# Low parts of the weights of layers 1 and 2: subtracted by GpSimd instead of DVE

## What is computed

```python
for i in range(n_layers):                       # 3 layers of 200 outputs
    z = jnp.einsum('bmd,bnd->bmnd', x, hidden).reshape(B, -1, D)
    cur = jnp.einsum('bcd,co->bod', z, Ws[i]) + bs[i][None, :, None]
    cur = jax.nn.relu(cur)
    if SPLIT_HALF and i != n_layers - 1:        # half goes on, half goes out
        hidden, direct = (cur[:, :half, :], cur[:, half:, :])
    else:
        direct = cur
        hidden = cur
    finals.append(direct)
return jnp.sum(jnp.concatenate(finals, axis=1), axis=-1)
```

## Time and profile before

| | |
|---|---|
| median of 3 runs | 2704.21 us (2703.4 to 2704.91) |
| the profiled execution | 2704.38 us |
| its span, first to last instruction | 2702.6 us |
| mean granted TensorE clock | 0.996 of full speed |
| TensorE busy | 2671.3 us, 99% |
| DVE busy | 2641.8 us, 98% |
| ScalarE busy | 1677.6 us, 62% |
| GpSimd busy | 3.3 us |

### The profile page before, as it was taken

How to read it: one execution, slowest core, us unless ns; L and a number is a source line. 1 busy time by engine, 2 the same in 40 slices (tenths; PEclk the granted TensorE clock), 3 DMA queues, 4 the chain that set the end, 5 groups by cost and what they waited for, 6 DMA issues and landing times.

```text
span 2702.6 us, 52144 instructions
## 1 busy us (share of the span) xinstructions
PE 2671.3 (99%) x17992; PEld 2658.1 (98%) x17992; DVE 2641.8 (98%) x2731; ACT 1677.6 (62%) x2853; POOL 3.3 (0%) x9
## 2 busy tenths in 40 slices
PE   6999999999999999999999999999999999999999
PEld 4999999999999999999999999999999999999999
DVE  6999999999999999999999999999999999999998
ACT  5666666666666666666666666666666666666664
POOL 0000000000000000000000000000000000000000
PEclk8999999999999999999999999999999999999999
DMA  8554444444554454444455444444444454445442
GB/s 196 131 145 129 110 115 131 121 110 123 135 139 112 127 131 110 114 130 123 112 134 142 121 110 125 130 113 113 129 127 114 119 133 118 110 125 130 112 110 63
DMA packets 230130, 332.65 MB, mean 123 GB/s; under 512 B 27976, under 2 KB 165172, under 8 KB 229940
## 3 DMA queue, kind: packets, MB, share of 16 engines
q1 hardware_dynamic: 230038, 331.46, 47.0%
HBM read 326.67 MB, written 6.60 MB: 123 GB/s over the span
## 4 chain that ended last, share of the span: by engine, by line
PE 97%; issue 1%; DVE 0%; DMA 0%; ACT 0%; SPq 0%; POOLq 0%; POOL 0%; ACTq 0%; DVEq 0%
PE acc L850 61%; PE acc L851 28%; PE acc L843 6%; PE turned L863 1%; PE x_turned L885 1%; PE x_turned L872 0%; DMA xb<-x_by_unit 0%; DVE z_low L483 0%; DVE w_split L434 0%; DMA mixed<-in_r_x_dram 0%; SPq L255 0%; ACT w_split L715 0%; DVE z L478 0%; ACT mixed L711 0%; POOLq L109 0%
## 5 line engine op out<-in xcount | busy, mean ns | idle before, releaser
L850 PE MATMUL acc<-w_split,z_high 128*128 128x400 f32 (+1 forms) x8320 | 2490.9, 367 | 19.4 <-DVE z_low L483 16.0
L851 PE MATMUL acc<-w_split,z_low 128*128 128x200 f32 (+1 forms) x8320 | 2119.4, 255 | 0.0
L851 PEld LDWEIGHTS acc<-w_split,z_low 128*128 128x128 f32 (+1 forms) x8320 | 1591.6, 191 | 0.0
L850 PEld LDWEIGHTS acc<-w_split,z_high 128*128 128x128 f32 (+1 forms) x8320 | 1564.0, 188 | 21.9 <-issue 16.4
L680 ACT ACTIVATE z_high<-z 128x1024 fp32r<-128x1024 f32 (+3 forms) x1152 | 1113.3, 976 | 693.2 <-DVE z L478 583.8
L483 DVE TENSOR_TENSOR z_low<-z,z_high 128x1024 fp32r<-128x1024 f32 (+3 forms) x1152 | 1284.7, 1115 | 26.5 <-PE acc L851 24.1
L478 DVE TENSOR_TENSOR z<-mixed,xb 128x1024 f32<-128x1024 f32 (+2 forms) x1024 | 1211.6, 1183 | 0.0
L705 ACT ACTIVATE mixed<-turned 32x128 f32<-32x128 f32 x768 | 205.5, 268 | 8.8
L843 PE MATMUL acc<-w_whole,z 128*128 128x200 f32 x1024 | 196.7, 335 | 0.8 <-DVE s L497 0.8
L843 PEld LDWEIGHTS acc<-w_whole,z 128*128 128x128 f32 x1024 | 168.1, 190 | 1.1 <-DVE s L497 1.1
L702 ACT ACTIVATE mixed<-turned 96x512 f32<-96x512 f32 x256 | 151.2, 590 | 6.9 <-PE turned L863 2.0
(11 more groups left out here) (27 smaller groups left out, 76.3 us busy)
## 6 DMA issues: line engine op xcount, KB each, us to landing
xb<-x_by_unit SPq DMA_DIRECT2D x378, 384.0 KB, 4.2
x_right<-x_by_unit SPq DMA_DIRECT2D x384, 136.5 KB
xb<-x_by_unit SPq DMA_DIRECT2D x384, 128.0 KB, 4.9
xb<-x_by_unit SPq DMA_DIRECT2D x126, 336.0 KB
xb<-x_by_unit SPq DMA_DIRECT2D x128, 84.0 KB
x_left<-x_by_unit SPq DMA_DIRECT2D x384, 19.5 KB
mixed<-in_L_rec_W_dram SPq DMA_DIRECT2D x5, 600.0 KB, 5.7
x_by_unit<-mixed SPq DMA_DIRECT2D x16, 160.0 KB, 2.9
```

Source lines behind the costliest of these rows:

```text
L850: nc.tensor.matmul(a[:, 0:2 * O], z_high[slot % HIGH_RING][0:rows, tok], w, start=(c == 0), stop=False, skip_group_check=True)
L851: last = nc.tensor.matmul(a[:, 0:O], z_low[slot % RING][0:rows, tok], w[:, 0:O], start=False, stop=(c == chunks - 1), skip_group_check=True)
```

## The change

The eight low parts of the weights of layers 1 and 2 are taken out of DVE's written order and put on GpSimd, between and around the two memsets of the staging buffer. The subtraction is the same, on the same tiles. DVE keeps the low part of the weights of layer 0. The orders of TensorE, ScalarE and SP are as before, and the counts keep their meaning.

```diff
--- before.py
+++ after.py
@@ -420,11 +420,24 @@
             pool.wait_ge(consts_step, 1)
             nc.gpsimd.affine_select(out=ident, in_=ident, compare_op=ALU.not_equal, fill=1.0,
                                     base=0, pattern=[[-1, P]], channel_multiplier=1).then_inc(consts, 1)
+            def low_piece(i, l, g):
+
+                pool.wait_ge(w_high_done, i + 1)
+                pool.wait_ge(w_low_done, i)
+                w = piece(l, g)
+                nc.gpsimd.tensor_tensor(w[:, :, O:2 * O], stage(l, g), w[:, :, 0:O].bitcast(F32), ALU.subtract).then_inc(w_low_done, 1)
+
+            pool.wait_ge(w_low_done, 1)
             for l in range(1, 3):
-
-                pool.wait_ge(w_low_done, 4 * l - 1)
+                at = GROUPS * (l - 1) + 1
+                low_piece(at, l, 0)
+                low_piece(at + 1, l, 1)
+
+                pool.wait_ge(w_low_done, at + 2)
                 nc.gpsimd.memset(stage(l, GROUPS - 1)[MAIN:P, :, :], 0.0).then_inc(stage_ready, 1)
-
+                pool.wait_ge(stage_ready, l)
+                low_piece(at + 2, l, 2)
+                low_piece(at + 3, l, 3)
 
         @block.vector
         def _(dve):
@@ -432,9 +445,6 @@
 
                 dve.wait_ge(w_high_done, i + 1)
                 nc.vector.tensor_tensor(w[:, :, O:2 * O], st, w[:, :, 0:O].bitcast(F32), ALU.subtract).then_inc(w_low_done, 1)
-
-            def low_piece(i, l, g):
-                low_w(i, piece(l, g), stage(l, g))
 
             def ones(i):
                 nc.vector.memset(xb[i][MAIN:P, TAIL_AT:CHUNKS, :], 1.0).then_inc(ones_set, 1)
@@ -548,11 +558,9 @@
             dve.wait_ge(w_low_done, 1)
             product0(0, 0, 0)
             lows(0, 0, L0_ROWS, L0_CHUNKS)
-            low_piece(1, 1, 0)
             sums(0, 1, 1, None)
             dve.wait_ge(s_in, 1)
             fresh(0, 1).then_inc(direct_in, 1)
-            low_piece(2, 1, 1)
 
 
             at = first(0)
@@ -565,21 +573,18 @@
             lows(at + 1, at + 1, P, group_chunks(1))
             sums(0, 1, 2, 1)
             product12(1, 0, 0, 3, at + 3, at + 3)
-            low_piece(3, 1, 2)
             product0(2, at + GROUPS, at + GROUPS)
             dve.wait_ge(s_in, 2)
             dve.wait_ge(direct_in, 1)
             add(0, 1).then_inc(direct_in, 1)
             lows(at + 2, at + 2, P, group_chunks(2))
             lows(at + 3, at + 3, P, group_chunks(3))
-            low_piece(4, 1, 3)
             lows(at + GROUPS, at + GROUPS, L0_ROWS, L0_CHUNKS)
 
 
             at = first(1)
             product12(1, 1, 1, 0, at, at)
             product12(1, 1, 1, 1, at + 1, at + 1)
-            low_piece(5, 2, 0)
             product12(1, 1, 1, 2, at + 2, at + 2)
             lows(at, at, P, group_chunks(0))
             sums(0, 2, ended(0), 2)
@@ -587,8 +592,6 @@
             product12(1, 1, 1, 3, at + 3, at + 3)
             lows(at + 2, at + 2, P, group_chunks(2))
             product0(3, at + 4, at + 4)
-            low_piece(6, 2, 1)
-            low_piece(7, 2, 2)
             lows(at + 3, at + 3, P, group_chunks(3))
             lows(at + 4, at + 4, L0_ROWS, L0_CHUNKS)
             product12(2, 0, 0, 0, at + 5, at + 5)
@@ -600,7 +603,6 @@
             product12(2, 0, 0, 3, at + 8, at + 8)
             sums(0, 2, ended(1), 3)
             lows(at + 7, at + 7, P, group_chunks(2))
-            low_piece(8, 2, 3)
 
             def period(r, d, n, base, sl):
```

## The result

The changed kernel takes 2719.82 us, median of 6 runs (2712.28 to 2720.53), against 2703.95 for the kernel before on the same chip: ratio 1.0052, 95% interval 1.0042 to 1.0062. It is 15.9 us slower. The six runs lie at two levels: 2712.28 and 2713.12, and four from 2719.75 to 2720.53. The forecast of 2712 was the lower level; most runs are on the upper one, outside the range. The profiled execution (2719.75 us, span 2717.9) is of the upper level.

What follows compares the result with a forecast made beforehand. TensorE runs without a break after a prologue up to 85.79 us, so only that start's shift counts. GpSimd and DVE shutting each other out move it by 8 us: 2704.2 + 8 = 2712 us, range 2705 to 2717.

Steps and rivals of the forecast that it cites:

- The price of a subtraction: GpSimd's time for one 128x1600 subtraction, worked out from memset and select rows: 3.5 us, bounds 1.4 and 4.8.
- The exclusion itself: In the prologue, DVE stands still during each GpSimd subtraction it overlaps, since both read two SBUF operands; taken as likeliest.
- The walk through the prologue: Step-by-step sum with engines excluding each other: TensorE starts at 43.12, 54.03 and 64.23 become 43.7, 55.2 and 67.0.
- piece 7's end at 78.1: Seventh subtraction on GpSimd, 74.7 to 78.1 us; the low part of 71.83 then done at 79.1, TensorE 6.5 us late.
- +2.2: Delay of TensorE's start at 85.79 if both engines run freely: it moves to 88.0 us.
- piece 8 in the exclusive sum: Eighth subtraction, 87.0 to 90.0 us, before group 2's low part; TensorE's group 3 starts 93.6 to 94, +8 us.
- whoever is ready first runs: Rule for GpSimd and DVE overlapping in the prologue: the first ready runs, the other waits for its end.
- slow clock: TensorE's clock falling to half after idle times; another such spell in the prologue could add 1.5 us.
- free sum: Prologue carried forward with GpSimd and DVE not hindering each other; the late seventh piece delays ScalarE's hidden values: +2.2 us.
- the free one: Rival: GpSimd and DVE do not hinder each other in the prologue; +2.2, 2706.5 us, chance 0.22.
- the partial one: Rival: both engines slower while they overlap, half of the exclusive cost; +4 to +6, 2709 us, chance 0.22.

Runs made afterwards that it cites:

- E3: Changed kernel with each GpSimd subtraction replaced by memsets of about its length, so GpSimd only writes; 2706.99 us, ratio 1.0012.
- E5: Changed kernel with DVE's sum of layers 0 and 1 of unit 1 moved behind the next unit's first product; 2712.53 us, ratio 1.0035.
- E9: The changed kernel run again with no edit; 2719.72 us (5 runs), its profiled execution at the lower level.
- E10: Kernel before with only the eighth subtraction on GpSimd and DVE's sum moved behind the next unit's first product; 2704.73 us, ratio 1.0004.
- E2: Kernel before with only the eighth subtraction moved to GpSimd, the other seven on DVE; 2712.76 us, ratio 1.0035.
- E4: Kernel before plus 24 probes, extra GpSimd subtractions of 128x800 into unused memory in the steady state; 2726.09 us.
- E7: Write-only kernel of E3 with the memset of layer 2's staging rows put behind the seventh piece; 2705.93 us, ratio 1.001.

## Why the prediction was wrong

**What held.** The price of a subtraction (3.5 us put down, 3.56 measured). The exclusion itself, by which DVE stands still (E3 against E5). The walk through the prologue: TensorE's starts were put at 43.7, 55.2 and 67.0 and are 43.85, 55.63 and 67.33; piece 7's end at 78.1 is 78.44. The sum gave 2712, and the runs of the lower level have it (2712.28, 2713.12, 2712.74); there group 3 starts at 94.73 (E9), where 93.6 to 94 was put down, although piece 8 holds the low part of group 3 and not that of group 2. A slip that changes nothing: +2.2 on 2704.2 is 2706.4, written once as 2707 and once as 2706.5.

**What failed** is one term, that of piece 8 in the exclusive sum: "Piece 8 (87.0 to 90.0) stands before the low part of group 2", and with it the sentence that whoever is ready first runs. It was 3.0 us by that sentence and is 10.94 (88.18 to 99.12). The instruction was ready at 88.18, DVE's next one began at 88.37, and DVE did seven in a row, to 96.1. The prediction took the exclusion as a queue in order of request. The probes show that it is not: a waiting GpSimd instruction does not get in between DVE's, in 24 cases of 24, until DVE comes to a sum, which reads one operand from PSUM and one from SBUF. Behind piece 8's request stood no sum, since it had just gone by, at 86.75. So everything waits for DVE to run dry, and DVE runs dry only because TensorE, which waits for the piece, frees no buffer. With the sum moved behind the request the turn comes at the sum (E5, E10). The price of that is 7.2 us, from E5 (2712.5) to E9 (2719.7). A part of it is the slow clock behind the gap of 6.60 us: the start of group 3 is 13.4 us later than before, the span 15.3 longer.

The Trainium skill (SBUF — State Buffer, § Who interferes with whom) was cited for the exclusion, and the first half of its rule is borne out: GpSimd's reads and DVE's two-operand instructions block each other, a write-only memset blocks nothing (E3). It also says that the port pair (a read and a write port that both engines use) is held for the whole instruction and that the order of issue decides who blocks. Pieces 2 to 7 show that in this trace; for a waiting GpSimd instruction beside a chain of DVE's, E2 (11.87 us) and E4 (up to 11.47 us) differ from it.

**Where the 15.9 us go.** The later pieces alone, with nothing excluded, cost 3.5 (E3, free sum 2.2), of which 1.1 goes when the memset stands behind piece 7 (E7). The exclusion at the eight pieces adds about 5.3 (E5's 8.8 less 3.5). The lost turn at piece 8 adds some 7. Each share holds what the clock did in its runs. Of the rivals, the free one was too low by 5 us and more in every run, and the partial one is not seen: the DVE instruction beside GpSimd's waits for its whole rest and then takes its usual time (39.62 to 42.71, with piece 2 ending at 41.62). The slow clock was put down as a possible +1.5 us on the side; in the changed kernel the matmuls behind the gaps of 2.20 us and more begin at 0.67 to 0.70 us each time, and no run has the price of that by itself.

**What stays open.** Pieces 3, 5, 6 and 7 got their turn at the next boundary of DVE's instructions, between two with two SBUF operands, where no probe ever did, and they did so in every trace that has them. So did piece 8 in E9. E9's had fresh idle time of DVE shortly before it; pieces 6 and 7 had none. What lets GpSimd in there was not settled. Nor was it tested that it is the operand in PSUM, and not something else in a sum, as its wait for ScalarE, that opens the turn. So the failed term is shown, and a whole rule in its place is not. Why a run takes the lower level is seen in one execution only, E9, where the clock stayed low longer and DVE ran out of work for a moment.

## What to carry to other kernels

Moving elementwise work from a full DVE to GpSimd gave nothing back here, where DVE's instructions read two SBUF operands: 12.7 us of DVE's work became some 26 us of GpSimd's, and DVE stood still for about 16 of them, beside pieces 2 to 7. If GpSimd must do such work beside a chain of DVE instructions, look for the next DVE instruction that has one of its two operands in PSUM; if none follows the request, the wait can be as long as DVE's lead, and a single short one moved behind the request was worth 7 to 8 us here. In pricing a resource that two engines share, ask not only how long each holds it but who gets it next.

## What the runs showed of the hardware that was not expected

- GpSimd with two SBUF operands beside a busy DVE in the steady state: 128x800 is about 1.9 us of work but takes 1.92 to 11.47 us from request to end (E4), and starts at DVE's sums with a PSUM operand, 24 times of 24.
- A write-only GpSimd costs DVE nothing: 1.23 us for a product with a memset beside it (E3), 3.09 with a subtraction (the changed kernel).
- The same program falls at two levels 7 us apart, by who wins one turn: its 11 runs lie at 2712.3 to 2713.1 (three) or at 2718.9 to 2722.1 (eight).
